# A graph network's attention: 95 gathers of rows of x1 become one-hot matmul lookups

## The reference

```
# first stage
zmax = max(x, axis=-1)
q      = 0.95 * zmax[src] * e[:, 1, :] + e[:, 0, :]
sum_q  = segment_sum(q, dst);  sum_ac = segment_sum(e[:, 1, :], dst)
z_new  = 0.2 * x + 0.8 * sum_q / (sum_ac + 1e-06)      # x where a node has no edge
x1     = layernorm(x + z_new)
# second stage: attention over the edges, 4 heads
Q, K, V = x1 Wq[h], x1 Wk[h], x1 Wv[h]
s       = Q[dst] . K[src] * 64**-0.5
alpha   = softmax of s over the edges of a receiver
agg     = segment_sum(alpha * V[src], dst), mean over the heads
out     = layernorm(x1 + (x1 + agg @ Wout))
```

## Time and profile before

| | |
|---|---|
| three timed runs | 2561.57, 2564.44, 2565.7 us |
| profiled execution, its own time | 2559.61 us |
| its span, first to last instruction | 2557.9 us |
| busy: TensorE, VectorE, ScalarE, GpSimd | 2040.9, 1727.1, 1313.3, 1881.4 us |
| mean granted TensorE clock | 0.743 of 2.4 GHz |

### The profile page before, as it was taken

The page is one execution under the profiler, slowest core; times in us unless marked ns, Lnnn a source line. Parts: engine busy times, 40 slices in busy tenths (PEclk is TensorE's granted clock), DMA queues, the critical chain, the costliest instruction groups (busy, mean ns, idle before and its releaser), DMA issues.

```text
span 2557.9 us, 75060 instructions
## 1 busy us (share of the span) xinstructions
PE 2040.9 (80%) x18960; PEld 1508.0 (59%) x18961; DVE 1727.1 (68%) x5572; ACT 1313.3 (51%) x3792; POOL 1881.4 (74%) x2347
## 2 busy tenths in 40 slices
PE   3999999878778877777887887787787878777886
PEld 3888888845555555545555555554565555554555
DVE  7999999786565555555665565555555666665567
ACT  5555555365454544544545545545545455554544
POOL 2888888777677777777777777777777777777750
PEclk9999999677576666677766667767757676777678
DMA  5787787312121212212122121221221212222111
GB/s 157 252 257 251 256 256 251 68 35 45 34 46 38 46 37 46 46 38 46 38 45 46 37 46 38 46 45 39 45 45 38 47 37 46 41 42 46 37 22 27
DMA packets 187098, 195.56 MB, mean 76 GB/s; under 512 B 106955, under 2 KB 109851, under 8 KB 184729
## 3 DMA queue, kind: packets, MB, share of 16 engines
q1 hardware_dynamic: 137278, 139.69, 19.7%
q0 software_dynamic: 49312, 50.59, 10.6%
HBM read 184.89 MB, written 5.25 MB: 74 GB/s over the span
## 4 chain that ended last, share of the span: by engine, by line
POOL 45%; PE 27%; issue 18%; DVE 4%; DMA 4%; ACT 1%; DVEq 0%; ACTq 0%; POOLq 0%; SPq 0%
POOL XS L632 43%; PE psVX L1376 4%; PE psN L1385 4%; PE psM L1385 4%; PE psS L1559 3%; DMA XS<-x_dram,dst_bs 3%; PE psVX L1514 2%; PE psM L1514 2%; PE psT L1509 1%; PE psA L1370 1%; PE psVX L1504 1%; PE psA L1524 1%; PE psA L1514 1%; PE psA L1450 1%; PE psS L1450 1%
## 5 line engine op out<-in xcount | busy, mean ns | idle before, releaser
L632 POOL DMA_INDIRECT XS<-x_dram,dst_bs x1516 | 1447.3, 955 | 473.3 <-issue 447.6
L926 DVE SCALAR_TENSOR_TENSOR l_st<-l_st,alpha,rsum 64x1 f32 x782 | 169.4, 217 | 515.8 <-PE psM L1514 268.1
L1559 PE MATMUL psS<-XT,Ubuf 96*128 96x512 f32 x522 | 416.3, 893 | 16.6 <-ACT Ubuf L1231 15.9
L1280 ACT COPY PmPT<-psT 128x512 f32<-128x512 f32 x196 | 114.9, 586 | 336.8 <-PE psT L1509 336.0
L998 DVE TENSOR_REDUCE rmax<-psS 128x1 f32<-128x512 f32 x391 | 270.5, 692 | 20.1 <-PE psS L1559 5.1
L1514 PEld LDWEIGHTS psVX<-XS,PmPT 128*128 128x128 f32 x1568 | 280.2, 267 | 1.6 <-ACT PmPT L1280 1.3
L1514 PE MATMUL psVX<-XS,PmPT 128*128 128x64 f32 x1568 | 279.7, 342 | 0.7 <-ACT PmPT L1280 0.7
L1504 PEld LDWEIGHTS psN<-ident,XS 128*128 128x128 f32 x366 | 55.2, 183 | 379.7 <-issue 379.2
L1504 PEld LDWEIGHTS psVX<-ident,XS 128*128 128x128 f32 x392 | 59.4, 183 | 365.7 <-issue 364.7
L1280 ACT COPY dst_bs<-psT 128x512 f32<-128x512 f32 x195 | 114.3, 586 | 301.2 <-PE psT L1509 300.2
L1514 PEld LDWEIGHTS psM<-XS,dst_bs 128*128 128x128 f32 x1464 | 262.4, 267 | 1.6 <-ACT dst_bs L1280 1.6
(11 more groups left out here) (286 smaller groups left out, 4220.8 us busy)
## 6 DMA issues: line engine op xcount, KB each, us to landing
big<-in_edge_attr_2x SPq DMA_DIRECT2D x342, 256.0 KB, 3.3
row_pair<-x_dram SPq DMA_DIRECT2D x2944, 0.2 KB
big<-dst_turned SPq DMA_DIRECT2D x49, 512.0 KB
XS<-x_dram,dst_bs POOLq DMA_INDIRECT x1516, 2.5
O<-in_edge_attr_2x SPq DMA_DIRECT2D x48, 256.0 KB, 3.3
O<-codes_dram SPq DMA_DIRECT2D x200, 6.0 KB
x_dram<-x SPq DMA_DIRECT2D x12, 128.0 KB, 2.0
out<-big SPq DMA_DIRECT2D x12, 128.0 KB
```

Source lines behind the costliest of these rows:

```text
L632: pool.indirect_dma_start(row_block(c, j), None, x1_dram, bass.IndirectOffsetOnAxis(ap=idx2[b % SB][:, k * CPP + j:k * CPP + j + 1], axis= ...
L926: dve.scalar_tensor_tensor(out=ls, in0=ls, scalar=al[half], in1=rs[half], op0=ALU.mult, op1=ALU.add)
L1280: act.copy(PTs[a][:, :], psT[:, :]).then_inc(pt_done, 1)
L1559: pe.matmul(psSc[1 - a][:, :], Ubuf[1 - a][:, :], XT[(J - 1) % 3][:, :], start=True, stop=True).then_inc(s_done, 1)
```

## The change

95 blocks are no longer gathered: the last block of every fourth chunk from chunk 12 on (chunk 12, 16, ... 388; `looked_up`). Their rows are looked up in x1 in SBUF. Before the loop x1 is split into three bf16 parts (`parts`, 7 slices x 3 parts x 448 columns), in the first seven passes, by ScalarE and VectorE in turns (`part_of`). A node is written as a code (its partition and its block // 7) and a lane (block % 7). `mean_and_codes` on VectorE works out the codes of all looked-up blocks; SyncE stores them to DRAM and loads one row of 128 codes at a time, spread over all partitions (`load_code`), two ahead.

A lookup takes four passes (a period, LE = 4). In the first VectorE compares the codes with 7 constants per partition, which gives 7 one-hot matrices of 128 x 128 in bf16 (`look_hot`). TensorE multiplies each with 3 parts of 448 columns, 21 matmuls that add up in psL (448 columns of psA), spread over nine places (`look`): 4 before the scores of the first pass, 2 in each of three places of the second and third, 2 and 3 in the fourth. Then VectorE multiplies by the lane mask and sums the seven lanes into the block's place in XS (`look_pick`). TensorE waits for it two passes later. A 96th lookup at the end fills a block that nobody reads.

What else moves: centring of x1 in place goes (the split table overwrites part of x1), so its mean is kept; at the end SyncE reads x1 back from x1_dram and GpSimd adds the negative mean in 13 steps (x1c), for which VectorE's L1084 waits. psA is now taken, so further visits use the transposes' bank, wait until it has been copied (u_done), and TensorE waits for the update after each visit. SyncE loads row numbers in 16 registers in place of 8, and issues its 64 rows of a block in two halves, each behind a code load that waits for the one-hot of two periods before. GpSimd writes two tables (iota) before its stage. The scratch for DMA descriptors is halved, from 8192 to 4096.

```diff
+    LE = 4
+    LG = 7
+    LW = LG * D
+    LC0 = H2 + 5
...
-    RR = 8
+    RR = 16
...
+    def blocks_gathered(c):
+        return CPP - 1 if looked_up(c) or by_row(c) and c != RC0 else CPP
...
+    def looked_up(c):
+        return c >= LC0 and (c - LC0) % LE == 0 and c < NCH
...
+    LP = ((0, 4), (4, 6), (6, 8), (8, 10), (10, 12), (12, 14), (14, 16), (16, 18), (18, 21))
...
+        tab_x1 = sb("tab_x1", [P, NB * D // 2 + NB * D])
+        parts = tab_x1[:, :].bitcast(BF16).rearrange("p (s k c) -> p s k c", s=LG, k=3)
+        x1 = tab_x1[:, NB * D // 2:]
...
+            def load_code(r, more):
+                row = code_dram[r:r + 1, :] if isinstance(more, int) else code_dram[bass.ds(more * LPI + r, 1), :]
+                sp.dma_start(code_b[r % 2], row.broadcast_to([P, P])).then_inc(l_code[r % 2], 16)
...
+            sp.wait_ge(s_lcode, 1)
+            sp.dma_start(code_dram, code_row[:, :]).then_inc(s_lcst, 16)
+            sp.wait_ge(s_lcst, 16)
+            sp.wait_ge(s_up, UG)
+            def codes_behind(b):
+                return range(-(-(S2 * b - 13) // LE), -(-(S2 * b - 5) // LE))
...
-                if b // 2 < RN:
-                    load_rows_of(b // 2, b % 2, more)
+                for k, r in enumerate(codes_behind(b)):
+                    sp.wait_ge(l_hot, r - 1 + more * LPI)
+                    load_code(r, more)
+                    if b // 2 < RN:
+                        load_rows_of(b // 2, (b % 2 * 2 + k, b % 2 * 2 + k + 1), more)
...
+            for r in range(codes_behind(NBL)[0], LN):
+                sp.wait_ge(l_hot, r - 1)
+                load_code(r, 0)
+            sp.wait_ge(l_sum, LN)
+            sp.dma_start(x1v[:, :, :], x1_dram.rearrange("(b p) d -> p b d", p=P)).then_inc(s_lcst, 16)
...
-                for j in range(CPP - 1 if by_row(c) and c != RC0 else CPP):
+                for j in range(blocks_gathered(c)):
...
+            pool.wait_ge(s_lcode, 1)
+            pool.wait_ge(s_lcst, 32)
+            for g in range(TG):
+                b0, nb = TB * g, blocks(g)
+                x_ = x1v[:, b0:b0 + nb, :]
+                pool.tensor_tensor(x_, x_, x1_mean[:, b0:b0 + nb].unsqueeze(2).broadcast_to([P, nb, D]), ALU.add).then_inc(s_x1c, 1)
...
+                if i is not None and (J - H2) % LE == LE - 1:
+                    look_pick(J, i)
...
-            def centre_x1(g):
-                b0, nb = TB * g, blocks(g)
-                x_, s_ = x1v[:, b0:b0 + nb, :], present_w[:, b0:b0 + nb]
-                link(dve.tensor_reduce(s_, x_, AX_X, ALU.add))
-                dve.scalar_tensor_tensor(out=x_, in0=s_.unsqueeze(2).broadcast_to([P, nb, D]), scalar=-1.0 / D, in1=x_,
-                                         op0=ALU.mult, op1=ALU.add)
+            def mean_and_codes():
+                dve.wait_ge(s_x1d, 16 * UG)
+                link(dve.tensor_reduce(x1_mean, x1v[:, :, :], AX_X, ALU.add))
+                link(dve.tensor_scalar(x1_mean, x1_mean, -1.0 / D, None, ALU.mult))
+                dve.wait_ge(s_lids, 16 * (RB + 1))
+                ids = look_ids.rearrange("r (p c) -> r p c", c=CPP)[:, :, CPP - 1]
+                link(dve.tensor_scalar(look_hi, ids, 7, None, ALU.logical_shift_right))
+                link(dve.tensor_scalar(look_s, look_hi, 37.0, None, ALU.mult))
+                link(dve.tensor_scalar(look_s, look_s, 8, None, ALU.logical_shift_right))
+                link(dve.scalar_tensor_tensor(out=lane_row, in0=look_s, scalar=-float(LG), in1=look_hi, op0=ALU.mult, op1=ALU.add))
+                link(dve.tensor_scalar(look_hi, ids, P - 1, None, ALU.bitwise_and))
+                link(dve.scalar_tensor_tensor(out=code_row[:, :], in0=look_s, scalar=float(P), in1=look_hi, op0=ALU.mult, op1=ALU.add))
+                dve.sem_inc(s_lcode, 1)
+
+            def keep_lanes():
+                dve.wait_ge(s_ltr, 1)
+                link(dve.tensor_copy(lane_col[:, :], psA[:, 0:LN]))
+
+            def part_of(k):
+                if k > 0:
+                    dve.wait_ge(s_tmid, k)
+                    dve.tensor_tensor(parts[:, k - 1, 2, :], hot_pick[:, :], parts[:, k - 1, 1, :], ALU.subtract).then_inc(s_tlo, 1)
+                    dve.wait_ge(s_tlo, k)
+                if k < LG:
+                    dve.wait_ge(s_thi, k + 1)
+                    dve.tensor_tensor(hot_pick[:, :], x1[:, k * LW:(k + 1) * LW], parts[:, k, 0, :], ALU.subtract).then_inc(s_trest, 1)
+
+            def look_hot(J, i):
+                r = (J - H2) // LE
+                q = r % 2
+                dve.wait_ge(l_code[q], 16 * (r // 2 + 1) + i * (8 * LPI))
+                dve.wait_ge(looked, r + 1 + i * LPI)
+                dve.tensor_tensor(hot.rearrange("p (s e) -> p s e", s=LG), code_b[q].unsqueeze(1).broadcast_to([P, LG, P]),
+                                  code_of.unsqueeze(2).broadcast_to([P, LG, P]), ALU.is_equal).then_inc(l_hot, 1)
+
+            def look_pick(J, i):
+                r = (J - H2) // LE
+                dve.wait_ge(l_sum, r + 1 + i * LPI)
+                dve.scalar_tensor_tensor(out=hot_pick[:, :], in0=lane_of, scalar=lane_col[:, bass.ds(i * LPI + r, 1)], in1=psL,
+                                         op0=ALU.is_equal, op1=ALU.mult).then_inc(l_pick, 1)
+                dve.wait_ge(l_pick, r + 1 + i * LPI)
+                dve.tensor_reduce(xs((LC0 + r * LE) % S2, CPP - 1), hot_pick[:, :].rearrange("p (l f) -> p f l", f=D), AX_X, ALU.add).then_inc(looked, 1)
...
                 attend(m, m, None)
+                if m == 0:
+                    mean_and_codes()
+                if m == 1:
+                    keep_lanes()
                 if m == 2:
                     centre_weights()
-                    dve.wait_ge(s_x1d, 16 * UG)
-                for g in range(TG):
-                    if m > 2 and g % 4 == m - 3:
-                        centre_x1(g)
+                if m > 0:
+                    part_of(m - 1)
+            part_of(LG - 1)
+            part_of(LG)
+            dve.wait_ge(s_const, 9)
             with nc.Fori(0, (NCH - H2) // U2, engines=(dve.engine,), hint_back_edge=True) as i:
                 for k in range(U2):
+                    if k % LE == 0:
+                        look_hot(H2 + k, i)
                     attend(i * U2 + (H2 + k), H2 + k, i)
             for m in range(NCH, NCH + 4):
...
+            def part_of(k):
+                if k > 0:
+                    act.wait_ge(s_trest, k)
+                    act.copy(parts[:, k - 1, 1, :], hot_pick[:, :]).then_inc(s_tmid, 1)
+                if k < LG:
+                    act.copy(parts[:, k, 0, :], x1[:, k * LW:(k + 1) * LW]).then_inc(s_thi, 1)
+
...
+            def look(J, i, place):
+                t = 3 * ((J - H2) % LE) + place - 2
+                if i is None or not 0 <= t < len(LP):
+                    return
+                first, end = LP[t]
+                if first == 0:
+                    pe.wait_ge(s_tlo, LG)
+                    pe.wait_ge(l_hot, (J - H2) // LE + 1 + i * LPI)
+                for n in range(first, end):
+                    last = pe.matmul(psL, hot[:, n // 3 * P:(n // 3 + 1) * P], parts[:, n // 3, n % 3, :], start=(n == 0), stop=(n == 3 * LG - 1))
+                if end == 3 * LG:
+                    last.then_inc(l_sum, 1)
...
                         xx = pe.snap(xv, min_val=1)
+                        pe.wait_ge(u_done, taken)
                         pe.wait_ge(x_mask, xx)
                         pe.wait_ge(x_u, xx)
-                        pe.matmul(psA[:, :], Ubuf[2][:, :], XT[J % 3][:, :], start=True, stop=True).then_inc(x_s, 1)
...
+                        weigh(J, PTX, psF[:, 0:D], x_pv)
                         pe.reg_add(xv, xv, 1)
+                        pe.wait_ge(x_upd, pe.snap(xv, min_val=2))
...
+                look(J, i, 0)
...
+                    if i is not None and (J - LC0) % LE == 0:
+                        pe.wait_ge(looked, (J - LC0) // LE + 2 + i * LPI)
                     pe.sem_inc(turn_steps, 1)
                     turn_rows(J, a)
                 if on(4):
                     pe.wait_ge(pt_done, vv)
                     weigh(J - 4, PTs[a], psVc[a][:, 0:D], pv_done)
+                look(J, i, 1)
                 if on(3):
                     pe.wait_ge(exp_done, vv)
                     turn_probs(Pms[1 - a], psT, tp_done)
-                    further_visits(J - 3)
+                    further_visits(J - 3, vv)
+                look(J, i, 2)
                 if on(1):
                     pe.wait_ge(mask_done, vv)
                     pe.wait_ge(u_done, vv)
```

86 lines of the change are left out of this document (67 added, 19 removed).

## The result

The changed kernel takes **2521.6 us** (median of 4 runs, 2517.6 to 2525.2) against 2564.9 for the kernel before on the same chip: a ratio of 0.9836, 95% interval 0.9824 to 0.9848, 43 us less. The forecast was 64 less, in a range of 2455 to 2565. The profiled execution took 2517.6 us, with a span of 2515.8.

A forecast was written before the change was run, and what follows sets the result against it. GpSimd's gathers set the pace of stage two. Gathers -119.6, comparison +20, start +5, visits +16, end +8, slow-clock spells +4 and tail +3 sum to -64 us, giving 2500 us from the median, range 2455 to 2565.

The forecast's parts named there:

- The gathers' term: Stage two, GpSimd: 95 gathers fewer at 1.26 us each, -119.6 us if GpSimd never waits.
- the longer gathers: Gathers beside VectorE's one-hot comparison last longer: 0.2 us for each of 96 comparisons, +20 us.
- rival 5: Lookup matmuls cost the ceiling of 0.384 us each on TensorE, 4.8 us a chunk at best; 2600 us, chance 0.02.
- rival 2: In stage two TensorE ties with GpSimd at 4.6 us a chunk and wins nothing back; 2540 us, chance 0.20.
- rival 3: TensorE's clock stays down in stage two, mean under 0.84, making the kernel slower; 2640 us, chance 0.10.
- rival 4: The comparison holds every gather beginning inside it until its end, 53 us in place of 20; 2533 us, chance 0.05.
- that of the further visits: Behind the 11 visits: GpSimd stops +16 us, spells at 1.2 GHz +4, later end of TensorE's chunks +8.
- GpSimd's reserve of "some 10 us": During a further visit GpSimd can run on some 10 us before it wants a slot back.
- TensorE's steady margin: Between visits TensorE at 2.4 GHz needs 4.15 us a chunk against GpSimd's 4.65, regaining 0.5 us a chunk.
- The clock: TensorE's granted clock in stage two would be 0.9 or more, with 16.6 of 18.6 us of work.
- My 0.8 us: TensorE's wait each period on VectorE, whose pick and next one-hot come almost back to back: 0.8 us.
- VectorE as "covered": VectorE's lookup work of 2.4 to 3.1 us a period fits, 16 of 18.6 us in use.

The follow-up runs named there:

- e7: Changed kernel with the one two-input comparison of 896 elements made as seven one-input comparisons of 128 elements; 2572.5 us.
- e9: Changed kernel with its comparison made as three two-input ones, TensorE's first lookup group waiting for the first of them alone; 2490.9 us.
- e1: Changed kernel with the 11 further visits left out on every engine; 2448.4 us.
- e4: Changed kernel with all 1541 gathers kept and the lookups computed in full, their sums put where nothing reads them; 2610.9 us.
- e5: Changed kernel with TensorE's wait for the visit's update moved from the visit's end to just before the next use of the shared bank; 2500.9 us.
- e3: Changed kernel with only the last of each lookup's 21 matmuls left; 2505.0 us.
- e8: Changed kernel with four more matmuls, whose result nobody reads, in each further visit; 2502.2 us.
- e11: Changed kernel with the visit's last wait moved, four more matmuls per visit, the first lookup group one place later and three shorter comparisons; 2460.9 us.

## Why the prediction was right, and where it was off

**The direction and the pace** were right. GpSimd set it: 1446 gathers in 1892 us, most of their idle time still "issue". The gathers' term (-118.6 for -119.6), the tail (+2.3 for +3) and the longer gathers (+16 for +20, the comparison scaled from the masks by the square) held; e7 and e9 confirm that the last one is the comparison and grows faster than its length, and the trace of before that the masks were the right thing to scale from. The lookup matmul took the floor, 0.19 us, so rival 5 is out. TensorE did not tie with GpSimd (15.7 us a period at full clock for 18.6, rival 2; the nearness to the forecast's 16.6 is in part luck, since the waits were 1.8 us and not 0.8, and the work of the four chunks was less than 4 x 2.8), the clock did not stay down (0.88, not under 0.84, rival 3), and the comparison did not hold gathers as rival 4 has it (16 us and not 53). The start cost nothing, where +5 stood.

**SyncE** at 0 was right: no stop in e1, where only visits are taken away and SyncE has its full load at the faster pace.

**The term that was mis-sized is that of the further visits**: +16 and +4 for stops, and +8 at the end, 28 in all; it measured 45 + 14 = 59. Three things were wrong in it.
- I took GpSimd's reserve of "some 10 us" as given. It goes by GpSimd's own pace, and shrinks when the pace rises. e4 shows 24 us of stops from the pace alone; the three and a half chunks that GpSimd can run on account for about 11 of them (an estimate), and the rest is open.
- I priced the new waits in a visit at 1 us and reckoned that most of it would vanish in the reserve. A visit is 1.8 us longer, 1.5 of it the wait at its end, and a visit that already uses up the reserve passes on every further microsecond: 21 us of stops at the old pace and 13 at the end (e4), 19 us back for moving one wait (e5).
- I took TensorE's steady margin, 0.5 us a chunk, as what decides how a visit is made good. e3 refutes it: with 20 of 21 matmuls gone the stops fell by 3 us.

**The clock** I forecast at 0.9 or more from the share of time with work; it was 0.88, and the missing part was not random: it fell in the waits inside visits (e8) and at the wait for the one-hot (e7, e9). My 0.8 us was for both waits on VectorE, the one behind the pick and the one for the one-hot. Where TensorE catches up they are 1.20 and 0.64, and their price is the waits and, where the clock falls, a slow chunk behind them.

**VectorE as "covered"** was too coarse. The lookup takes it 2.7 us a period (2.4 to 3.1 forecast), and by busy time 2.3 to 3.0 us of room were left; e7 used 0.4 us more, and its stops grew by 63 us. The room was in the sum over a period, and the one-hot and the new maximum are each wanted at one point of it.

What stays open: how much of e5 and e8 is the shorter visit and how much the clock behind it, as they come together in every visit (the visits are 17.8 us shorter in sum for 19 us of time in e5, and 10.9 for 18 in e8, so behind e8's there is more); half of the 24 us that the faster pace costs; what moving VectorE's pick behind the new maximum would bring; and the stops of e11 (15 us) and its end (19 us against 8 without visits) were not taken further.

## What to carry to other kernels

Where a producer runs ahead through a ring, its reserve is the steps that it may run ahead of the one in work (three and a half here, not the eight slots) times its own pace: a change that speeds it up thins the reserve, so look in the trace for the rare long steps that it has to bridge, and price every microsecond added to them in full and as often as they come. On a TensorE with a clock that follows its work, count a wait twice, once for itself and once for what runs slowly behind it, and don't count on taking matmuls away. An engine that is "covered" by its busy share can still be late at one point: find the instruction that the others wait for, and make its first part short. Look, too, for what the engine does ahead of it and could do later (not tried here).

## What was not expected of the hardware

- Taking 1838 of 8051 matmuls out of 1800 us moved TensorE's busy time by 42 us, the granted clock going from 0.88 to 0.71 (e3).
- Four matmuls that do nothing, in a wait of 2.1 us, made the kernel 18 us faster (e8).
- Waits of 1.21 and 1.01 us were followed by a chunk of 6.83 us at 1.2 GHz (e7), where after waits of 1.20 and 0.64 the same chunk of a period takes 3.55 at 2.4 (changed kernel).
- The same 896 elements compared in three two-input instructions cost the gathers 22 - 15 = 7 us beyond the level of before, in one instruction 17, and in seven one-input instructions nothing; those took 281 ns for 128 elements each and started 0.2 us apart. But the one-input masks of 0.50 us, too, lengthen the gathers beside them, by 36 ns each (kernel before).
